# Attention kernel on one core: x normalised on ScalarE, v's low part on GpSimd, a warm-up, joined key halves, values 22 steps behind

## The reference

```python
h = jnp.maximum(_layernorm(x, axis=-1), 0.0)        # eps 1e-5
q = h @ Wq.T + bq
k = h @ Wk.T + bk
v = h @ Wv.T + bv
a = q @ k.T / sqrt(256) + adj + adj
out = x + softmax(a, axis=-1) @ v
```

## Time and profile before

| | us |
|---|---|
| median of 3 runs (lowest, highest) | 862.66 (862.32, 863.13) |
| the profiled execution, its own time | 862.07 |
| its span in the trace | 860.0 |
| TensorE (matmuls) busy | 819.8 |
| VectorE busy | 592.9 |
| GpSimd busy | 394.8 |
| ScalarE busy | 343.5 |
| 16 DMA engines, mean busy share | 31.1% of the span |

### The profile page before, as it was taken

One profiled execution on the slowest core, in us unless ns is written; L12 is line 12 of the kernel. 1 busy time (PEld: TensorE's weight loads), 2 busy tenths in 40 slices (PEclk: granted clock), 3 DMA queues, 4 the chain that ended last, 5 costly groups with the idle time before them and its releaser, 6 DMA issues.

```text
span 860.0 us, 16570 instructions
## 1 busy us (share of the span) xinstructions
PE 819.8 (95%) x6720; PEld 816.4 (95%) x6720; DVE 592.9 (69%) x986; ACT 343.5 (40%) x616; POOL 394.8 (46%) x325
## 2 busy tenths in 40 slices
PE   5766899999999999999999999999999999999998
PEld 4766799999999999999999999999999999999998
DVE  4455586767777776767777776767777677767764
ACT  2221234444434444444434344443444344443455
POOL 4255354452709082543618081634528090725445
PEclk9988899999999999999999999999999999999999
DMA  4225023232324332333323332333323243423200
GB/s 158 85 70 199 10 76 96 89 111 86 113 74 123 99 111 86 98 105 94 111 74 115 95 123 87 110 88 98 104 81 114 84 123 94 116 86 92 82 26 13
DMA packets 43708, 81.68 MB, mean 95 GB/s; under 512 B 4976, under 2 KB 5616, under 8 KB 43632
## 3 DMA queue, kind: packets, MB, share of 16 engines
q1 hardware_dynamic: 43632, 80.63, 31.1%
HBM read 76.42 MB, written 4.19 MB: 94 GB/s over the span
## 4 chain that ended last, share of the span: by engine, by line
PE 90%; POOL 4%; DVE 3%; ACT 1%; issue 1%; DMA 1%; SPq 0%; DVEq 0%; ACTq 0%
PE ps L276 44%; PE ps L362 14%; PE ps L364 14%; PE ps L363 14%; POOL x_rows L236 4%; PE ps L268 1%; DVE stats L481 1%; PE ps L342 1%; POOL rstd L231 1%; DVE ring_a L512 1%; DVE hT L491 1%; DMA x_rows<-in_x 1%; PE ps L349 0%; ACT hT L409 0%; DVE mean_var L484 0%
## 5 line engine op out<-in xcount | busy, mean ns | idle before, releaser
L276 PE MATMUL ps<-qhl,hT 128*128 128x256 f32 x3072 | 409.3, 283 | 0.1
L276 PEld LDWEIGHTS ps<-qhl,hT 128*128 128x128 f32 x3072 | 386.2, 191 | 0.3 <-DVE v L506 0.3
L252 POOL TENSOR_TENSOR ring_a<-ring_a,m_row 128x512 f32<-128x512 f32 x179 | 230.6, 1340 | 276.6 <-ACT m_row L460 276.6
L362 PE MATMUL ps<-v,p_hi 128*128 128x258 f32 x1024 | 291.2, 284 | 1.2 <-DVE x_res L551 1.2
L364 PE MATMUL ps<-v,p_lo 128*128 128x258 f32 x1024 | 288.7, 282 | 0.0
L363 PE MATMUL ps<-v,p_hi 128*128 128x256 f32 x1024 | 288.6, 282 | 0.0
L456 ACT CAST p_hi<-ps 128x512 fp32r<-128x512 f32 x256 | 150.4, 588 | 231.4 <-PE ps L364 229.4
L512 DVE TENSOR_TENSOR ring_a<-ps,ring_a 128x512 f32<-128x512 f32 x179 | 123.6, 690 | 104.3 <-PE ps L276 103.6
L362 PEld LDWEIGHTS ps<-v,p_hi 128*128 128x128 f32 x1024 | 193.9, 189 | 1.5 <-DVE x_res L551 1.4
L364 PEld LDWEIGHTS ps<-v,p_lo 128*128 128x128 f32 x1024 | 194.0, 189 | 0.0
L363 PEld LDWEIGHTS ps<-v,p_hi 128*128 128x128 f32 x1024 | 193.4, 189 | 0.0
(11 more groups left out here) (63 smaller groups left out, 357.9 us busy)
## 6 DMA issues: line engine op xcount, KB each, us to landing
ring_a<-in_adj SPq DMA_DIRECT2D x179, 256.0 KB, 2.6
ring_b<-in_adj SPq DMA_DIRECT2D x77, 256.0 KB, 2.6
x_res<-in_x SPq DMA_DIRECT2D x16, 256.0 KB, 2.9
out<-x_res SPq DMA_DIRECT2D x16, 256.0 KB, 2.0
x_rows<-in_x SPq DMA_DIRECT2D x7, 512.0 KB, 3.7
x_rows<-in_x SPq DMA_DIRECT2D x4, 128.0 KB, 3.2
w_all<-in_w SPq DMA_DIRECT2D x1, 512.0 KB, 4.4
w_all<-in_w SPq DMA_DIRECT2D x1, 256.0 KB, 4.4
```

Source lines behind the costliest of these rows:

```text
L252: nc.gpsimd.tensor_tensor(slot_tiles(w), slot_tiles(w), m, ALU.subtract).then_inc(s_sub, 1)
L276: last = nc.tensor.matmul(dst, lhs(a, ib), rhs(c, ib), start=(n == 0), stop=(n == 3 * DB - 1))
L362: nc.tensor.matmul(ps[:, O_BANK + i, 0:VW], hi, v[:, n, 0:VW], start=(n == 0), stop=False)
```

## The change

- `normalize` for groups 2 to 7 runs on ScalarE (one activation for a tile, x * rstd + offset, offset = -mean * rstd made by GpSimd), group 1 and half of group 0 on VectorE, the other half of group 0 on ScalarE.
- `v_lo` runs on GpSimd. Since it reads a copy in SBUF, ScalarE writes that copy too (`v_full`), and the bank is free for the next projection after `v_hi`.
- A third buffer for x (`x_third`); the load of group g waits for the transposes of group g - 3.
- Wq, Wk and the bias columns are loaded by ScalarE's queue in three transfers, ahead of its table load.
- 14 transposes of the identity are TensorE's first work (WARM).
- `h_hi` and `h_lo` take both halves (128 x 1024) in one instruction; for group 0 only `h_lo` does.
- The first groups are interleaved in another order: one projection of v stands between the two of q.
- `running_max` of a block's last step is followed by a maximum over the two key halves (128 x 256), and `turn_max` transposes 2 pieces in place of 4; the reduction reads 128 x 256.
- LAG is 22, and at step 251 (HOLD) no values are weighed, so that from there on they are 23 behind.
- The loads of adj for the ring's last two slots wait for the last `v_lo`.

```diff
-    LAG = UNITS + 4
+    LAG = UNITS + 6
+    HOLD = (STEPS - 5,)
+    WARM = 14
+    XB = 3
...
+        def due(s):
+            return None if s in HOLD else s - LAG - sum(h < s for h in HOLD)
...
             def load_x(g):
-                if g >= 2:
-                    sp.wait_ge(s_ht, DB * (g - 2) + DB)
-                sp.dma_start(x_rows[:, g % 2], x_groups[g]).then_inc(s_x[g % 2], 16)
+                if g == 2:
+                    sp.wait_ge(s_g, 1)
+                if g >= XB:
+                    sp.wait_ge(s_ht, DB * (g - XB + 1))
+                sp.dma_start(rows(g), x_groups[g]).then_inc(s_x[g % XB], 16)
...
-            for s in range(FIRST, RING):
+            sp.wait_ge(s_ht, DB * (GROUPS - 2))
+            for s in range(FIRST, RING - 2):
+                load_adj(s)
+            sp.wait_ge(s_vlo, 2 * GROUPS)
+            for s in range(RING - 2, RING):
                 load_adj(s)
...
+            def v_lo(g, pair):
+                pool.wait_ge(s_vhi, 2 * g + pair + 1)
+                t = GT * g + 2 * pair
+                nc.gpsimd.tensor_tensor(v[:, t:t + 2, VW:VW + D], v_full[:, pair], v[:, t:t + 2, 0:D].bitcast(f32),
+                                        ALU.subtract).then_inc(s_vlo, 1)
...
+            for g in range(GROUPS):
+                v_lo(g, 0)
+                v_lo(g, 1)
+                if g + XB < GROUPS:
+                    make_rstd(g + XB)
...
+            for _ in range(WARM):
+                nc.tensor.transpose(ps[:, X_BANK, 0:P], ident[:, :], ident[:, :])
...
                 for i in range(QS):
-                    for k in range(KT):
-                        last = nc.tensor.transpose(ps[:, X_BANK, (i * KT + k) * P:(i * KT + k + 1) * P],
-                                                   acc[:, k * QB + i * P:k * QB + (i + 1) * P], ident[:, :])
+                    last = nc.tensor.transpose(ps[:, X_BANK, i * P:(i + 1) * P], max_rows[:, i, :],
+                                               ident[:, :])
...
+            for g in range(1, GROUPS):
                 if g + 1 < GROUPS:
                     transpose_h(g + 1)
-                if g > 0:
-                    pe.wait_ge(s_hlo, DB * g + DB)
+                pe.wait_ge(s_hlo, g + 1)
                 project_v(g, 0)
                 scores(2 * g)
...
-            act.wait_ge(s_wqk, 16)
             for w in range(2):
+                nc.scalar.dma_start(w_all[:, w * DB * D:(w + 1) * DB * D], w_pack[:, w * DB * D:(w + 1) * DB * D])\
+                    .then_inc(s_w[w], 16)
...
+            def normalize(g, tiles):
+                act.wait_ge(s_off, g + 1)
+                for j in tiles:
+                    last = nc.scalar.activation(rows(g)[:, j], rows(g)[:, j], ACT.Identity,
+                                                bias=offset[:, g % XB, j:j + 1], scale=rstd[:, g % XB, j:j + 1])
+                return last
...
             def v_hi(g, pair):
                 act.wait_ge(s_vmm, 2 * g + pair + 1)
+                if g > 0:
+                    act.wait_ge(s_vlo, 2 * (g - 1) + pair + 1)
                 t = GT * g + 2 * pair
                 at = ps[:, V_BANKS[pair]:V_BANKS[pair] + 2, :]
+                nc.scalar.copy(v_full[:, pair], at[:, :, 0:D])
                 nc.scalar.copy(v[:, t:t + 2, 0:D], at[:, :, 0:D])
...
+                    dve.wait_ge(s_acc, b + 1)
+                    if b > 0:
+                        dve.wait_ge(s_bcast, b)
+                    halves = acc[:, :].rearrange("p (k i n) -> p k i n", k=KT, i=QS)
+                    nc.vector.tensor_tensor(max_rows[:, :, :], halves[:, 0], halves[:, 1], ALU.max)\
+                        .then_inc(s_cols, 1)
...
-            for s in range(FIRST, STEPS + LAG):
+            for s in range(FIRST, STEPS + LAG + len(HOLD)):
                 b, u = s // UNITS, s % UNITS
-                if LAG - 1 <= s < STEPS + LAG - 1:
-                    write_p_hi(s - LAG + 1)
+                if s not in HOLD and 0 <= due(s) + 1 < STEPS:
+                    write_p_hi(due(s) + 1)
```

More of the change, by code:

```diff
@@ L177, in store @@
                 sp.dma_start(out[b], x_res[:, :, :]).then_inc(s_out, 16)
[L179 to L183, removed]
+            for j in range(GT):
+                sp.dma_start(rows(0)[:, j], x_groups[0, :, j]).then_inc(s_x0[j], 16)
             sp.dma_start(w_all[:, 2 * DB * D:], w_pack[:, 2 * DB * D:WB]).then_inc(s_wv, 16)
-            sp.dma_start(bias_cols[:, :], b_pack).then_inc(s_bc, 16)
             load_x(1)
@@ L438, in _ @@
             q_hi(0)
+            act.wait_ge(s_wlo, 1)
+            v_hi(0, 0)
             q_hi(1)
-            for g in range(GROUPS):
+            h_hi(1)
+            v_hi(0, 1)
+            normalize(2, range(GT)).then_inc(s_norm, 1)
+            for g in range(1, GROUPS):
                 if g + 1 < GROUPS:
@@ L553, in finish @@
                 last.then_inc(s_fin, 1)
-            group_stats(0)
+            for j in range(GT // 2):
+                tile_stats(0, j)
             for w in range(2):
@@ L559, in _ @@
                                         ALU.subtract).then_inc(s_nlo, 1)
-            dve.wait_ge(s_rstd, 1)
-            for j in range(GT):
-                last = nc.vector.tensor_scalar(x_rows[:, 0, j], x_rows[:, 0, j], mean_var[:, 0, j, 0:1],
-                                               rstd[:, 0, j:j + 1], ALU.subtract, ALU.mult)
-            last.then_inc(s_norm, 1)
+            for j in range(GT // 2, GT):
+                tile_stats(0, j)
+            group_stats(0)
             dve.wait_ge(s_bc, 16)
@@ L573, in _ @@
                                            G[:, 0].bitcast(f32), ALU.mult, ALU.subtract).then_inc(s_glo, 1)
+            normalize(0, range(GT // 2))
+            for j in range(GT):
+                tile_stats(1, j)
+            group_stats(1)
             h_lo(0)
@@ L577, in _ @@
                                     wv_T[:, 0, :, D:VW].bitcast(f32), ALU.subtract).then_inc(s_ulo, 1)
+            normalize(1, range(GT))
             q_lo(0)
+            for j in range(GT):
+                tile_stats(2, j)
+            group_stats(2)
             q_lo(1)
-            for g in range(GROUPS):
+            h_lo(1)
+            for j in range(GT):
+                tile_stats(3, j)
+            add_adj(0)
+            group_stats(3)
+            for g in range(1, GROUPS):
                 if g + 1 < GROUPS:
                     h_lo(g + 1)
-                if g > 0:
-                    add_adj(2 * g - 1)
-                if g + 2 < GROUPS:
-                    group_stats(g + 2)
-                v_lo(g, 0)
-                if g > 0:
-                    running_max(2 * g - 1)
+                add_adj(2 * g - 1)
+                if g + XB < GROUPS:
+                    for j in range(GT):
+                        tile_stats(g + XB, j)
+                running_max(2 * g - 1)
+                if g + XB < GROUPS:
+                    group_stats(g + XB)
                 add_adj(2 * g)
-                v_lo(g, 1)
                 running_max(2 * g)
             add_adj(FIRST - 1)
-            for s in range(FIRST, STEPS + LAG + 1):
+            for s in range(FIRST, STEPS + LAG + len(HOLD) + 1):
                 b, u = s // UNITS, s % UNITS
-                if s - LAG >= UNITS and (s - LAG) % UNITS == 0:
-                    finish((s - LAG) // UNITS - 1)
+                if s not in HOLD and due(s) > 0 and due(s) % UNITS == 0:
+                    finish(due(s) // UNITS - 1)
                 if s - 1 < STEPS:
@@ L602, in _ @@
                     reduce_max(b - 1)
-                if LAG - 1 <= s < STEPS + LAG - 1:
-                    write_p_lo(s - LAG + 1)
+                if s not in HOLD and 0 <= due(s) + 1 < STEPS:
+                    write_p_lo(due(s) + 1)
                 if s < STEPS:
```

139 lines of the change are left out of this document (82 added, 57 removed).

## The result

| | us |
|---|---|
| median of 4 runs (lowest, highest) | 823.57 (822.90, 823.66) |
| kernel before, on the same chip | 862.75 (862.32, 863.13) |
| ratio, 95% interval | 0.9544 (0.9528 to 0.9561) |
| the profiled execution, its own time and its span | 823.64, 821.8 |

What follows compares the result with a forecast made beforehand. TensorE was taken as the bound, full after about 110 us but waiting on GpSimd's normalisation in the prelude. Prelude -34.7, turns -3.2, last block +0.2: 862.07 - 37.7 = 824.4, median 825.0 us; range 819 to 833.

Steps and rivals of the forecast that it cites:

- What bounds the kernel: Whole kernel: TensorE full from about 110 us; in the prelude it waited 22.6 us for GpSimd's normalisation, with a falling clock.
- Start: Kernel start: G begins at 7.45 us, 1.5 earlier; first projection of q at 18.4, still at 1.2 GHz.
- The warm-up at nothing gained: Kernel start: the 14 transposes do not raise TensorE's clock, so they save nothing.
- clock up early: Rival, kernel start: warm-up or earlier weights raise the clock before G; about -5 us, 820; chance 0.12.
- Groups 0 and 1, the wait of 2 us: Early prelude: TensorE waits 2 us for ScalarE's cast and normalisation; transposes of group 2 begin at 31.9.
- Groups 1 to 6: Prelude: TensorE sets the pace at 6.6 us a group; six groups take 39.6 us, to 71.5.
- The collision of the running maximum: Prelude: one of two running maxima a group takes 1795 ns beside GpSimd's subtraction; VectorE needs 6.4 of 6.6 us, hidden.
- the rival in which VectorE sets the pace: Rival, prelude: VectorE or GpSimd slower than TensorE, some 1.1 us a group, 5 to 7 in all, 831; chance 0.20.
- Last group to first values: Prelude's end: scores(16) at 78.6 us after a wait of 1.4 for `v_lo`; first values at 89.5.
- The turns: Block ends: two transposes fewer save 0.21 us a turn, 3.2 us in 15 blocks; the last block +0.2.
- LAG and HOLD: Steady stage: LAG 22 and the held step move work and take none away; later slot loads stay hidden.
- The sum: Whole kernel: 862.07 - 37.7 gives 824.4 us for the profiled execution, 825.0 for the median.

Runs made afterwards that it cites:

- numbers 1: Changed kernel with groups 2 to 7 normalised on GpSimd and v's low part written by VectorE again, third x buffer kept: 827.48 us.
- 2: Changed kernel with two x buffers in place of three, statistics one group less far ahead, engines as in the change: 840.26 us.
- number 12: Version with 24 warm-up transposes, Wq and Wk in one transfer on SyncE's queue behind two tiles of x: 821.92 us.
- Number 7: Changed kernel with 24 warm-up transposes in place of 14: 820.81 us.
- number 5: The changed kernel run again unedited, as a control: 823.06 us (820.84 to 824.52).
- number 9: Version with 24 warm-up transposes, without the maximum over the two key halves, so the turn has 4 transposes: 824.35 us.
- numbers 3: Changed kernel without the maximum over the two key halves, so the turn has 4 transposes: 824.79 us.
- numbers 4: Changed kernel with LAG 20 and no held step: 821.54 us.
- 10: Version with 24 warm-up transposes, LAG 20 and no held step: 821.75 us.
- number 11: Version with 24 warm-up transposes, group 2 normalised ahead of v(0,1)'s high part, last `v_lo` on VectorE from PSUM: 817.81 us.
- numbers 6: Changed kernel without the 14 warm-up transposes: 825.07 us.
- 8: Changed kernel with 14 f32 matmuls of the identity as warm-up in place of the 14 transposes: 822.03 us.

## Why the prediction was right, and where it was not

**What bounds the kernel**: right. TensorE's idle time in the prelude was the gain, and numbers 1 and 2 show which part of the change took it: mainly the third buffer with the statistics a group further ahead (23.0 of 27.3 us alone), less the engines (10.5 alone). The prediction costed the whole order and did not say this; nothing in it tells the two apart.

**Start**: G forecast at 7.45, measured 6.82; q(0) at 18.4, measured 17.65: 0.6 and 0.75 early. The two casts lay apart (4.38 and 5.42), as the weights landed in two parts, where the prediction took Wk's landing alone, at about 6.1. Its bracket of 0 to 1.5 us more from a split queue holds the 0.6; number 12 gives 0.9 for queue, split and order together.

**The warm-up at nothing gained**: this step failed. It rested on two rows of 2.90 us after mixed activity, which say nothing of transposes, and on the rule of the Trainium skill ("TensorE: Matmul & The Clock Gate", Part 4) that transposes do not count. Number 7 refutes that rule for f32 transposes: 1.70 us for G behind 24 of them, 2.90 without. In the profiled execution of the change G and q(0) still ran cold, at the late end of what this start does, so the sum was hit all the same, and that is luck: over the six profiles of this start q(0) begins within 3.3 us, which fits the spread from 820.8 to 824.5 of number 5. The rival "clock up early" was given 0.12 and 820. Number 7 comes near it in time, at 820.81, first values 2.7 us earlier (86.19), but gets there by half of its mechanism: G and the bias terms ran warm, q(0) cold again (2.90 us from 14.63), so it gave under 3 us and not 5.

**Groups 0 and 1, the wait of 2 us**: right, 1.85 us at 31.18, against 31.9 forecast. One term was mis-sized: the normalisation on ScalarE took 597 ns, the upper end, not the 472 taken; four of them took 2.07 us, not 1.7:

```profile
L460 ACT ACTIVATE x_pair<-x_pair,offset,rstd 128x256 f32<-128x256 f32 x18 | 9.4, 594 | 0.3
...
L460 ACT ACTIVATE x_third<-x_third,offset,rstd 128x256 f32<-128x256 f32 x8 | 4.2, 597 | 0.1
```

The row of 472 ns had one column operand (the bias), this one has two (scale and bias); it also read PSUM, where this one reads SBUF, and no run separates the two. The Trainium skill ("ScalarE: Activation LUTs", What ACT_TABLE_LOAD costs) gives 186 ns + 0.833 ns an element and 93 ns more for each column operand: an estimate of 585 ns for 256 elements and two operands. The trace agrees within 2%, and had it been used it would have picked the upper end. It would have counted on the path at group 2 only, and there the forecast happened to hold it: the prediction's terms (28.6 + 1.25 + 1.7) add up to 31.55, not to the 31.9 that it states, and the 0.35 between them is what the longer normalisation took.

**Groups 1 to 6**: 6.6 forecast, 6.62 measured; busy times forecast 5.3 (ScalarE), 5.3 (VectorE), 4.4 (GpSimd) against 5.24, 5.29 and 4.40. The collision of the running maximum with GpSimd's `v_lo` was over-sized: one of two a group was expected near 1795 ns, and in the prelude two of 14 come near it (1.57 us at 61.68, 1.56 at 68.29). Of the 14 that read two operands in SBUF the mean is 862 ns:

```profile
L263 POOL TENSOR_TENSOR v<-v_full,v 128x512 fp32r<-128x512 f32 x16 | 20.1, 1259 | 22.2 <-ACT row_terms L480 22.1
...
L587 DVE TENSOR_TENSOR acc<-acc,ring_a 128x512 f32<-128x512 f32 x14 | 12.1, 862 | 0.4
```

In the group from 37.85 on none of them is longer than 0.69 us, and where one is, the pace stays 6.6 us: it is hidden. So the rival in which VectorE sets the pace, given 0.20, did not come true.

**Last group to first values**: scores(16) at 78.6 after a wait of 1.4; measured 78.00 and 1.16. The forecast's own terms give 1.16 (1.25 + 1.34 - 1.43), not 1.4; in the trace `v_lo` took 1.19 and not 1.34, and the hand-overs between the engines took about that much more. The 0.6 us that the prelude came out ahead of the forecast (88.93 for 89.5) are the early start: from q(0) to the first values it is 71.28 us, where 71.1 were forecast.

**The turns**: 3.2 us forecast in 15 blocks, 3.5 measured by number 9, with 0.2 us a block in the timelines of numbers 3 and 9. **LAG and HOLD** neutral: numbers 4 and 10 agree, by the steady stage of their traces more than by their times. The longer way of a slot round the ring starved nothing: median landing 2.7 us now, and no wait of the scores for adj in the list of waits.

**The sum**: 824.4 forecast for the profiled execution, 823.64 measured; 825.0 for the median, 823.57. The mechanism of the prelude and of the turns was right; that the start came out within 1 us rests on the moment at which the clock rose.

## What to carry to other kernels

When an engine waits for a chain of small steps at every group, ask how early the chain can start before asking which engine is faster: one more buffer and statistics one group further ahead gave 23.0 of the 27.3 us of groups 2 to 7, and the other engines alone gave 10.5 and left 9.99 us a group where 6.6 were possible. Read a price for a moved operation from a row with the same number of column operands and the same source memory. And where the clock's chance at the start is as large as the effect, compare a stage of the trace that lies behind it (here five blocks of the steady stage), or price the change on a version whose clock behaves more alike in each execution.

## What the runs showed of the hardware

- **The clock fell with a gap and without one, and at different moments of one and the same work.** In number 7 G ran warm from 6.70, TensorE waited 0.94 and 2.09 us in what followed, and q(0) ran cold again. In number 11 TensorE did not wait, and the transposes behind G and the bias terms were cold all the same (1.94 us, 1.07 in number 7):

```profile
11.02 1.94 PE L302 MATMUL ps<-ident,x_pair 128*128 128x128 f32 x8
```

Behind the wait of 1.85 us before the transposes of group 2 the clock fell in the profiles of numbers 6, 8 and 10 (8.2 to 8.3 us to the next transposes) and not in seven others with the same wait (6.7). What decides it is not shown. Windows of number 7, 12 to 14 us and q(0) itself, the column before the last two being the granted clock:

```profile
12.00:14.00 2.00, 0.54 (x5) 0.30 (x3) 1.13 (x6) 1.09 (x2) 1.32 (x3) 0.72 0.66 224
...
14.63:17.32 2.69, 2.69 (x12) 2.69 (x13) 1.21 (x4) 0.00 (x0) 0.00 (x0) 0.50 0.76 285
```

- **The page's clock can be silent at the start.** In the profile of the change q(0) takes 2.90 us from 17.65, as it does above at 0.50, but the window shows the full clock, as all windows of this trace do. In number 6 q(0) takes 2.90 us under a column of 1.00 as well, and the column first changes behind 31 us. So at the start the distance between matmuls tells the clock, not the column:

```profile
18.00:19.00 1.00, 1.00 (x6) 1.00 (x6) 0.86 (x3) 0.00 (x0) 0.00 (x0) 1.00 1.01 379
```

- **Small operations on GpSimd have no small price.** 1/sqrt of 128x4 numbers takes 1.03 us, nearly as long as the subtraction of 128x512 (1.19 to 1.34 us); minus_mean took 0.19 us in one kernel and 0.65 in another.
